# Graph layers over a dense count matrix: node rows as whole fp32 stationary operands in place of two float32r parts

## The reference

```python
# layer 2, four times, with ReLU
norm = dinv[row] * dinv[col]              # self-loops are added to the edges
h = x @ W
out = segment_sum(h[row] * norm[:, None], col, n) + b
# layer 3, twice
agg = segment_sum(x[src], dst, n)
h = relu((x + agg) @ Wa + ba)
h = h @ Wb + bb
# after each of both layers
x = layernorm(x_before + h)
```

## Time and profile before

| what | value |
|---|---|
| time, median of three runs | 5514.3 us (5514.03 to 5519.43) |
| span of the profiled execution | 5520.0 us |
| instructions in it | 100522 |
| `dense`, first adjacency load to last result store issued | 3303.88 to 5488.63 us |
| casts in `dense`, all three engines | 17 x 119 = 2023 |

### The profile page before, as it was taken

The page is one execution under the profiler, slowest core; times in us unless marked ns, Lnnn a source line. Parts: engine busy times, 40 slices in busy tenths (PEclk is TensorE's granted clock), DMA queues, the critical chain, the costliest instruction groups (busy, mean ns, idle before and its releaser), DMA issues. The chain is left out here.

```text
span 5520.0 us, 100522 instructions
## 1 busy us (share of the span) xinstructions
PE 4387.9 (79%) x24072; PEld 3677.8 (67%) x24073; DVE 3584.6 (65%) x7941; ACT 2265.8 (41%) x4134; POOL 2783.0 (50%) x2730
## 2 busy tenths in 40 slices
PE   7566776766567776777658839999999999999997
PEld 4455555554234444444347739999999999999996
DVE  4888888885478888888786675444445654443443
ACT  0333333332135555555326644444444443344332
POOL 0477777773057777777421104444444443344432
PEclk8788888886877777777779959999999999999998
DMA  1444444442157777777425534343434432233332
GB/s 43 123 117 116 117 117 116 118 116 76 43 164 195 197 199 200 198 200 197 123 76 155 156 94 155 133 163 140 151 143 161 174 142 107 102 143 135 137 124 73
DMA packets 543158, 750.83 MB, mean 136 GB/s; under 512 B 57967, under 2 KB 441966, under 8 KB 542734
## 3 DMA queue, kind: packets, MB, share of 16 engines
q1 hardware_dynamic: 461182, 521.35, 28.1%
q0 software_dynamic: 81552, 224.63, 15.0%
HBM read 584.36 MB, written 161.41 MB: 135 GB/s over the span
## 5 line engine op out<-in xcount | busy, mean ns | idle before, releaser
L577 POOL DMA_INDIRECT arena<-table_kv,arena x1664 | 1738.5, 1045 | 652.6 <-issue 506.4
L2321 PE MATMUL ps<-moving,parts 128*128 128x384 f32 (+1 forms) x11662 | 2017.0, 332 | 38.0 <-ACT moving L2383 20.4
L2321 PEld LDWEIGHTS ps<-moving,parts 128*128 128x128 f32 x11662 | 1950.5, 189 | 71.7 <-ACT moving L2383 29.4
L2262 POOL CAST moving<-counts 128x1152 fp32r<-128x1152 uint8 (+1 forms) x420 | 476.7, 1135 | 739.6 <-PE ps L2321 609.8
L340 ACT ACTIVATE counted<-ps 128x392 uint8<-128x392 f32 x1568 | 665.5, 503 | 335.2 <-PE ps L331 298.7
L2262 POOL CAST moving<-big 128x1152 fp32r<-128x1152 uint8 (+1 forms) x413 | 468.4, 1134 | 608.7 <-PE ps L2321 608.7
L331 PE MATMUL ps<-by_place,by_lo 128*128 128x392 bf16 x1568 | 631.3, 525 | 107.1 <-DVE by_place L295 77.1
L687 PE MATMUL ps<-arena 128*128 128x137 f32 x1664 | 328.0, 355 | 335.6 <-DVE arena L821 313.1
L2383 ACT ACTIVATE moving<-counts 128x1152 fp32r<-128x1152 uint8 (+1 forms) x360 | 366.9, 1024 | 437.3 <-PE ps L2321 434.4
L2383 ACT ACTIVATE moving<-big 128x1152 fp32r<-128x1152 uint8 (+1 forms) x354 | 360.4, 1023 | 429.2 <-PE ps L2321 429.0
L687 PEld LDWEIGHTS ps<-arena 128*128 128x128 f32 x1664 | 280.0, 245 | 365.9 <-ACT arena L732 216.9
(11 more groups left out here) (329 smaller groups left out, 5343.1 us busy)
## 6 DMA issues: line engine op xcount, KB each, us to landing
counts<-adjacency SPq DMA_DIRECT2D x53, 2352.0 KB, 8.5
big<-adjacency SPq DMA_DIRECT2D x52, 2352.0 KB, 8.4
adjacency<-slots SPq DMA_DIRECT2D x784, 98.0 KB
edge_values<-arena SPq DMA_DIRECT2D x208, 256.0 KB, 3.3
arena<-edge_values SPq DMA_DIRECT2D x208, 256.0 KB, 3.1
arena<-table_kv,arena POOLq DMA_INDIRECT x1664
big<-table_norm SPq DMA_DIRECT2D x60, 192.0 KB, 5.6
big<-adjacency SPq DMA_DIRECT2D x7, 1568.0 KB, 6.4
```

What stands on the lines that cost most here:

```text
L577: pool.indirect_dma_start(m.ring4[r][:, k * 2 * D:(k + 1) * 2 * D], None, table, bass.IndirectOffsetOnAxis(m.src[:, j * HALF + k:j * HALF ...
L2262: pool.tensor_copy(to, of).then_inc(by_pool, 1)
L2321: mm = pe.matmul(m.bank(g % 2, n * P), d.parts[SOURCE[u]][:, s + q, t_, :], moving[:, q * n * P:(q + 1) * n * P], start=(s + q == 0 and t_ ...
```

## The change

The `parts` buffers, the masking and the three operations that fill them are gone. Rows are kept whole in fp32, in three buffers `d.rows`: two new ones, and `rest`, which already held the layer's input. `SOURCE` and `TARGET` say which of them a unit reads and writes; the step that finishes an item's rows writes them there itself. `moving` has the type fp32 in place of float32r. The product over a source block is one fp32 product. The counts, the casts and their shares, the items, groups and loads are as before.

Waits: in the first item of a unit TensorE waits on the semaphore of the step that wrote the rows (`rowed`, `lned`, `relued`) in place of `high` and `low`. For `gin_left`, ScalarE copies the sum at k = 0 in place of k = 4, straight into the rows, after a wait on `stored`. The norm rows have buffers of their own.

```diff
-SOURCE = (0, 1, 0, 1, 0, 1, 0)
-KEPT_BITS = 12
+SOURCE = (2, 0, 1, 0, 1, 0, 2)
+TARGET = (0, 1, 0, 1, 0, 1, None)
...
-        self.moving = [sb(f"moving{k}", GROUP * CHUNK, F32R) for k in range(MOVING)]
-        self.parts = [sb(f"parts{k}", BLOCKS * 2 * P, F32R)[:, :].rearrange("p (b t f) -> p b t f", t=2, f=P) for k in range(2)]
+        self.moving = [sb(f"moving{k}", GROUP * CHUNK) for k in range(MOVING)]
         self.rest = m.big[:, 0:BLOCKS * P]
+        self.rows = [sb(f"dense_rows{k}", BLOCKS * P)[:, :] for k in range(2)] + [self.rest]
...
+        def rows_of(of, b, n):
+            return d.rows[of][:, b * P:(b + n) * P]
+
+        def made(u, b, n):
+            return rows_of(TARGET[u], b, n)
...
-                    if fresh:
-                        pe.wait_ge(high, upto("high", u * CUTS + holding(s + some - 1)))
-                        pe.wait_ge(low, upto("low", u * CUTS + holding(s + some - 1)))
+                    if fresh and u == 0 and k == 0:
+                        pe.wait_ge(padded, 7)
+                    if fresh and u in (1, 2, 3):
+                        pe.wait_ge(rowed, upto("rowed", (u - 1) * CUTS + holding(s + some - 1)))
...
                     for q in range(some):
-                        for t_ in range(2):
-                            mm = pe.matmul(m.bank(g % 2, n * P), d.parts[SOURCE[u]][:, s + q, t_, :],
-                                           moving[:, q * n * P:(q + 1) * n * P],
-                                           start=(s + q == 0 and t_ == 0), stop=(s + q == BLOCKS - 1 and t_ == 1))
+                        mm = pe.matmul(m.bank(g % 2, n * P), rows_of(SOURCE[u], s + q, 1), moving[:, q * n * P:(q + 1) * n * P],
+                                       start=(s + q == 0), stop=(s + q == BLOCKS - 1))
...
-                if kind == "gin_left" and k == 4:
+                if kind == "gin_left" and k == 0:
                     act.wait_ge(eaten, (g + 1) * len(SHARES))
-                    act.wait_ge(low, upto("low", e))
-                    act.activation(rows_of(b, n), y, ACT.Copy).then_inc(copied, 1)
+                    act.wait_ge(stored, 16 * upto("stored", e))
+                    act.activation(made(u, b, n), y, ACT.Copy).then_inc(copied, 1)
...
-            def cutting(rows, n, e):
...
-            def lower(rows, u, b, n, e):
...
-                    cutting(h, n, e)
-                if kind == "gcn" and k == 8:
-                    lower(h, u, b, n, e)
...
-            for e in range(4):
-                first(e)
             fill(0)
```

More of the change, by code:

```diff
@@ L2057 @@
 CUTS = len(chunks())
[L2058 to L2063, removed]
+ITEMS = [(u, kind, b, n) for u, kind in enumerate(UNITS) for b, n in chunks()]
+SIGNALS = {"gcn": "scaled relued projected rowed",
+           "gcn_end": "scaled relued projected rowed aggregated rooted inverted lned stored",
+           "gin": "copied hidden relu0 relu1 projected rowed relued",
+           "gin_left": "copied",
            "gin_right": "copied hidden relu0 relu1 projected rowed rested aggregated rooted inverted lned stored"}
@@ L2129, in dense @@
     names = ("params_in turned_norm norm_copied norm_out padded counts_in0 counts_in1 norm_in0 norm_in1 x_in0 x_in1 "
-             "whole by_act by_dve by_pool eaten scaled relued projected rowed cut high low aggregating aggregated rooted "
+             "whole by_act by_dve by_pool eaten scaled relued projected rowed aggregating aggregated rooted "
              "inverted lned stored copied hidden relu0 relu1 rested missed peaked spotted flagged")
@@ L2133, in dense @@
             block, params_in, turned_norm, norm_copied, norm_out, padded, counts_in0, counts_in1, norm_in0, norm_in1,
-            x_in0, x_in1, whole, by_act, by_dve, by_pool, eaten, scaled, relued, projected, rowed, cut, high, low,
+            x_in0, x_in1, whole, by_act, by_dve, by_pool, eaten, scaled, relued, projected, rowed,
             aggregating, aggregated, rooted, inverted, lned, stored, copied, hidden, relu0, relu1, rested, missed, peaked,
@@ L2137, in dense @@
         counts_in, norm_in, x_in = (counts_in0, counts_in1), (norm_in0, norm_in1), (x_in0, x_in1)
-        total = len(ITEMS) - CUTS
-        unit_ends = {u: (u + 1) * CUTS - 1 for u in range(len(UNITS) + 1)}
+        total = len(ITEMS)
         params = 9
         def item(g):
-            u, kind, b, n = ITEMS[g + CUTS]
-            return u - 1, kind, b, n, g + CUTS
+            return *ITEMS[g], g
         def seen(name, g):
-            return sum(1 for k in range(g + 1) if k % 2 == g % 2 and ITEMS[k + CUTS][1] in name)
+            return sum(1 for k in range(g + 1) if k % 2 == g % 2 and ITEMS[k][1] in name)
         def group(k):
@@ L2218, in store @@
                     sp.dma_start(tables["x"][b * P:(b + n) * P, :].rearrange("(b p) f -> p b f", p=P),
-                                 d.h[:, 0:n * P].rearrange("p (b f) -> p b f", f=P)).then_inc(stored, 16)
+                                 made(u, b, n).rearrange("p (b f) -> p b f", f=P)).then_inc(stored, 16)
                 if kind == "gin_right":
@@ L2286, in step @@
                         else:
-                            pe.matmul(hid[:, o, 0:width], d.w2a[:, 0, c], rows_of(b, n), start=True, stop=False)
+                            pe.matmul(hid[:, o, 0:width], d.w2a[:, 0, c], made(u - 1, b, n), start=True, stop=False)
                             mm = pe.matmul(hid[:, o, 0:width], d.w2a[:, 1, c], d.a[:, 0:width], start=False, stop=True)
@@ L2313, in _ @@
                     s, some = group(k)
-                    if fresh:
-                        pe.wait_ge(high, upto("high", u * CUTS + holding(s + some - 1)))
-                        pe.wait_ge(low, upto("low", u * CUTS + holding(s + some - 1)))
+                    if fresh and u == 0 and k == 0:
+                        pe.wait_ge(padded, 7)
+                    if fresh and u in (1, 2, 3):
+                        pe.wait_ge(rowed, upto("rowed", (u - 1) * CUTS + holding(s + some - 1)))
+                    if fresh and u == 4:
+                        pe.wait_ge(lned, upto("lned", (u - 1) * CUTS + holding(s + some - 1)))
+                    if fresh and u == 5:
+                        pe.wait_ge(relued, upto("relued", (u - 1) * CUTS + holding(s + some - 1)))
                     pe.wait_ge({"a": by_act, "d": by_dve, "p": by_pool}[who], mine(who, g, k))
@@ L2334, in _ @@
         def _(act):
[L2335 to L2338, removed]
             def step(g, k):
@@ L2356, in step @@
                     two = d.h[:, 0:2 * width].rearrange("p (b o f) -> p b o f", o=2, f=P)
-                    act.activation(rows_of(b, n).rearrange("p (b f) -> p b f", f=P), two[:, :, 1, :], ACT.Relu)
-                    act.activation(d.half[:, 0:width].rearrange("p (b f) -> p b f", f=P), two[:, :, 0, :],
+                    act.activation(rows_of(SOURCE[u + 2], b, n).rearrange("p (b f) -> p b f", f=P), two[:, :, 1, :], ACT.Relu)
+                    act.activation(made(u, b, n).rearrange("p (b f) -> p b f", f=P), two[:, :, 0, :],
                                    ACT.Relu).then_inc(relued, 1)
@@ L2428, in normalized @@
                 for c in range(n):
-                    last = dve.tensor_scalar(d.h[:, c * P:(c + 1) * P], d.half[:, c * P:(c + 1) * P], d.two[:, c, 0:1],
+                    last = dve.tensor_scalar(to[:, c * P:(c + 1) * P], d.half[:, c * P:(c + 1) * P], d.two[:, c, 0:1],
                                              d.inverse[:, c:c + 1], ALU.subtract, ALU.mult)
@@ L2443, in step @@
                     dve.wait_ge(projected, upto("projected", e))
-                    wait(dve, low, upto("low", e - 1))
-                    dve.tensor_tensor(h.rearrange("p (b f) -> p b f", f=P), turned.rearrange("p (b f) -> p b f", f=P),
+                    rows = made(u, b, n).rearrange("p (b f) -> p b f", f=P)
+                    dve.tensor_tensor(rows, turned.rearrange("p (b f) -> p b f", f=P),
                                       copies(m.norm[:, b:b + n], 2, P), ALU.mult).then_inc(rowed, 1)
-                    dve.wait_ge(rowed, upto("rowed", e))
                     if u == 0:
-                        dve.scalar_tensor_tensor(d.missed[:, b:b + n], h.rearrange("p (b f) -> p b f", f=P)[:, :, HID], -1.0,
+                        dve.wait_ge(rowed, upto("rowed", e))
+                        dve.scalar_tensor_tensor(d.missed[:, b:b + n], rows[:, :, HID], -1.0,
                                                  m.degree[:, b:b + n], ALU.add, ALU.mult).then_inc(missed, 1)
-                    cutting(h, n, e)
-                if kind == "gcn" and k == 8:
-                    lower(h, u, b, n, e)
                 if kind == "gcn_end" and k == 7:
@@ L2459, in step @@
                 if kind == "gcn_end" and k == 12:
[L2460 to L2465, removed]
+                    normalized(made(u, b, n), n, e)
                 if kind in ("gin", "gin_right") and k == 5:
@@ L2471, in step @@
```

(5 more changed lines are left out.)

28 lines of the change are left out of this document (3 added, 25 removed).

## The result

The changed kernel takes 7130.76 us (median of four runs, 7126.09 to 7132.30); the kernel before took 5516.67 in the runs beside it (5514.03 to 5519.43). The ratio is 1.2927, with a 95% interval of 1.2906 to 1.2948. The forecast was 7136, slower, in a range of 7095 to 7195.

The account below looks back on a forecast made before the run. TensorE's stream of products was taken to fill 99% of the dense stage. Span 5520.0 + 1665 (products) - 33 (listed waits) - 10 (short hesitations) = 7142 us; with the median 5.7 us lower, 7136, range 7095 to 7195.

Parts of the forecast that it names:

- The bound: Dense stage, 2170.7 us: TensorE's stream of products fills it to 99%, so a product's cost there is the change's worth.
- The price: Dense-stage products on TensorE: one fp32 product at 0.645 or 0.430 us replaces two at 0.3466 or 0.240; 1665 us more.
- Weight loads: TensorE in the dense stage: two loads a block as before, costing nothing; 2216 us at most if cover were lost.
- The three operations: Masking, copying and subtracting on VectorE and ScalarE, beside TensorE: worth only the waits they cause, 7.3 us for VectorE.
- The waits: TensorE's dense-stage waits for ScalarE and VectorE casts: 33 us go, plus an estimated 10 us of unlisted short hesitations.
- `gin_left`'s moved copy: ScalarE's copy moved to k = 0: covered like the other copies, as TensorE needs the queued cast 1.94 us later.
- Starts of units: TensorE's waits for the previous unit's last rows before k = 15 and 16: nothing, up to some us over five units.
- Earlier stages: Stages before the dense one keep their instructions; another length of one would be a sign of being wrong.
- rival 1: Dense-stage fp32 products: the second record is hidden by the first, giving the old pair's price and 5471 us; chance 0.02.
- rival 2: Dense-stage fp32 products: each is one record instead of two, giving 5325 us; chance 0.01.
- rival 4: Dense stage: the clock falls in the longer stream, each tenth at 1.2 GHz adding 361 us, some 7500; chance 0.03.
- rival 3: Dense stage: TensorE's waits stay, or unit starts cost as much as is won, giving 7179 us; chance 0.06.

Follow-up runs that it names:

- doubled stream: The changed kernel with a second fp32 product a block on a zero stationary operand, adding nothing to the sums: 10754.16 us (one run).
- kept operations: The kernel before with masking, copying and subtracting kept, but fp32 parts and casts and one fp32 product a block: 7127.4 us, ratio 1.2937.
- old price: The changed kernel with float32r rows and casts and two products a block: 13532.65 us with sums counted twice, 5524.52 us with the second product's stationary operand zero.
- casts reordered: One float32r product a block in the new arrangement, three adjacency and six moving buffers, GpSimd casting each item's first three groups: 4812.23 us, ratio 0.8729.
- lower product left out: The kernel before with one float32r product a block, the lower part's product omitted, masking, copying and subtracting kept: 4947.93 us, ratio 0.8948.

## Why the prediction was right

*The bound.* The stage was read rightly as TensorE's stream of products; its rise of 1614.5 us (3785.2 - 2170.7) is the change.

*The price.* Forecast 0.645 and 0.430 us a product, found 0.645 and 0.431. 5145 x 0.645 + 686 x 0.431 = 3614 us, against 10290 x 0.1733 + 1372 x 0.120 = 1948 before: 1666 us more, where the forecast had 1665. The doubled stream confirms it to a microsecond.

*Weight loads.* As many as before, and forecast at nothing. The 0.645 us of a product hold its two loads, in the steps as in the stream, and in the doubled stream with its 24265 loads nothing comes on top.

*The three operations.* Forecast at nothing but for VectorE's waits. Keeping them changes nothing (3784.5 against 3785.2 us).

*The waits.* Forecast 33 us listed and 10 unlisted; by the difference, 1666 - 1614.5 = 51.5 us went. The term was a little small in its unlisted part: from start to start of the records, the stream before lost some 36 us at the listed waits and 17 at 159 delays of about 0.1 us that the view does not list. The largest group of these, 67, stands where the forecast had looked for it, in the first four units at the third group of an item, which VectorE casts behind its scaling. That the length of a group and not the removed work did nearly all of it is what the runs with kept operations and with the old price show; at the old price the 159 delays are there too. There the waits for VectorE did go with the work, 6 us, which the forecast put down to it. One reading of it was off without harm: of the 35 waits for ScalarE 33 stand at the starts that it names, one in the first item and one in the last item but one.

*`gin_left`'s moved copy.* Forecast covered, and it is; at the old price it makes 17 waits.

*Starts of units.* Forecast at nothing; TensorE's list has no wait for rows.

*Earlier stages.* Forecast unchanged. The first dense product came at 3303.4 us in place of 3314.3, which the forecast had named as a sign of being wrong. But the first load of adjacency rows in `dense` went out at 3292.84 in place of 3303.88, so the first product follows it after 10.5 us now and 10.4 before: the 11 us lie ahead of `dense`, where everything stands that was changed. In the other runs the first product came between 3296.7 (casts reordered) and 3322.6 (lower product left out), so they belong to the execution. With the 7.5 us by which the stage was shorter than forecast, less 0.7 that the tail was longer, they make the 17.7 us by which the profiled span, 7124.3, is under the forecast 7142.

*Luck.* That the median is only 5 us under the forecast is in part luck. The forecast took 5.7 us off the span to come to a median, as the profiled execution of the kernel before was longer than its median run. That of the changed kernel was its shortest, and its span lies 6.5 us under the median. This makes up for 12 of the 17.7 us.

*The rivals.* Two records a product, 0.3226 us apart, and a clock of 1.00 leave nothing of rivals 1, 2 and 4; the list of waits, empty but for the last item, rules out rival 3. By the Trainium skill ("TensorE: Matmul & The Clock Gate", section "Back-to-back issue gap") products of 512 columns come about 131 ns apart in a stream of loads and products, closer than the about 216 of isolated ones. This is not seen here: fp32 records of 384 columns stay 0.3226 us apart in 7.4 ms of stream, and bf16 products of 384 columns 0.1625.

## What to carry to other kernels

Price a change of operand type by the distance of starts in an undisturbed stream of the same type and width; here the steps and the planning stage of the same trace held one. The length of a record and the number of matmul calls both mislead. Here one whole fp32 product cost nearly twice as much as the two float32r products that it replaced. Work beside a bound engine can be removed for nothing, and waits can vanish without it: ask how long the covering work lasts before crediting an edit with a wait.

## What the runs showed that I had not expected

Two bf16 products a block cost 11 ns each less than float32r ones of the same width (0.1625 against 0.1733 us), with loads of 98 ns against 188. And the dense stage follows TensorE only down to some point between 2049 us (two bf16 products) and 1535 us (one float32r product): in the latter a third of the saved products' time came back, most of it as waits for casts.
